# The next batch's Mamba preparation moved from the FFN to the end of attention, 16 scan halves in the FFN, and the squares summed by VectorE

## The reference, cut to what matters

```python
# x (4, 512, 512), ctx (4, 512, 256); every norm is a layernorm without weights
attn = softmax(q k^T / sqrt(32)) v @ Wo   # 16 heads, mixed with a "splat" term from distances to 8 points per head
x1 = layernorm(x + attn)
# cross part, a Mamba scan over the context; 512 channels, 16 states
u = silu(causal_conv4(in_proj @ ctx) + conv_b)
dt_lo, Bm, Cm = split(x_proj @ u)         # 16 + 16 + 16 rows
delta = softplus(dt_proj @ dt_lo + dt_bias)
for n in range(16):                       # per channel, a scan over 512 steps
    state_n[t] = exp(delta[t] * A_n) * state_n[t-1] + delta[t] * u[t] * Bm[n, t]
    y += state_n * Cm[n]
x2 = layernorm(x1 + (y + D * u) * silu(x1))
h = silu(x2 @ Wg) * (x2 @ Wu)             # 2048 wide, ternary weights
out = layernorm(x2 + rms_norm(h) @ Wp)
```

## Time and profile before

| | us |
|---|---|
| median of three runs (lowest, highest) | 1603.4 (1598.43, 1607.87) |
| the profiled execution | 1601.84 |
| its span, first to last instruction | 1599.4 |
| mean granted clock of TensorE | 0.845 of full |

### The profile page before, as it was taken

The page is one execution under the profiler, slowest core; times in us unless marked ns, Lnnn a source line. Parts: engine busy times, 40 slices in busy tenths (PEclk is TensorE's granted clock), DMA queues, the critical chain, the costliest instruction groups (busy, mean ns, idle before and its releaser), DMA issues.

```text
span 1599.4 us, 14040 instructions
## 1 busy us (share of the span) xinstructions
PE 1217.3 (76%) x4602; PEld 571.0 (36%) x4602; DVE 1214.2 (76%) x1425; ACT 744.9 (47%) x1102; POOL 256.7 (16%) x299
## 2 busy tenths in 40 slices
PE   5664747779599857789689858788889856776895
PEld 4332212223345413333445423233445422222453
DVE  5868978789829895789739885889649886889423
ACT  6674424434457533444467423444376424443231
POOL 1000222001112231001112231011112221001111
PEclk8766976779799988789899977889799978788798
DMA  6843893556249795456259793455249693555253
GB/s 195 277 156 105 185 225 88 119 127 136 72 120 213 172 216 143 93 118 133 79 126 214 165 224 115 104 125 134 66 124 230 155 212 103 114 121 114 66 140 90
DMA packets 116759, 228.54 MB, mean 143 GB/s; under 512 B 14560, under 2 KB 25312, under 8 KB 116688
## 3 DMA queue, kind: packets, MB, share of 16 engines
q1 hardware_dynamic: 89248, 144.95, 31.6%
q0 software_dynamic: 26496, 81.80, 26.9%
q10 hardware_dynamic: 944, 0.92, 0.2%
HBM read 116.08 MB, written 29.62 MB: 91 GB/s over the span
## 4 chain that ended last, share of the span: by engine, by line
DVE 32%; PE 27%; DMA 17%; issue 8%; ACT 4%; SPq 2%; POOL 1%; DVEq 0%; ACTq 0%; POOLq 0%
DVE ST L854 10%; PE ps L1432 8%; DMA qk_parts<-PT 5%; DVE ST L846 5%; PE ps L1402 5%; PE ps L1240 4%; DVE MX L910 4%; DMA RD<-PT 4%; DMA RD<-QAK 3%; PE ps L1257 3%; DVE ST L857 3%; DVE BST L890 2%; DMA KS<-qk_parts 2%; DMA YA<-ST 2%; SPq L349 2%
## 5 line engine op out<-in xcount | busy, mean ns | idle before, releaser
L854 DVE TENSOR_TENSOR_SCAN ST<-dA,ST 128x1024 f32<-128x1024 f32 x128 | 316.5, 2473 | 14.9 <-ACT dA L556 11.5
L1240 PE MATMUL ps<-KS,QS 96*128 96x512 f32 x256 | 139.7, 629 | 150.2 <-DVE MX L910 78.3
L910 DVE TENSOR_REDUCE MX<-ps 128x1 f32<-128x512 f32 x256 | 165.0, 685 | 110.6 <-PE ps L1240 110.5
L1432 PE MATMUL ps<-V,GU 128*128 128x512 f16 x1024 | 241.3, 391 | 6.4 <-DVE V L1031 5.6
L457 POOL DMA_DIRECT2D YA<-ST x128 | 112.3, 877 | 790.1 <-DVE ST L857 765.0
L556 ACT ACTIVATE dA<-DL,Aneg 128x511 f32<-128x511 f32 x256 | 168.8, 713 | 97.0 <-DVE ST L854 96.7
L687 ACT ACTIVATE PT<-ps 128x1024 f32<-128x1024 f32 x128 | 125.2, 1019 | 124.2 <-PE ps L1346 123.5
L846 DVE TENSOR_TENSOR ST<-DU,BC 128x1024 f32<-128x1024 f32 x128 | 155.8, 1217 | 13.4 <-DMA BC<-bc_rows 8.0
L857 DVE TENSOR_TENSOR ST<-ST,BC 128x1024 f32<-128x1024 f32 x128 | 159.4, 1245 | 4.4
L1402 PE MATMUL ps<-WP,QS 128*128 128x512 f32 x512 | 144.7, 426 | 14.7 <-DVE QS L1045 13.0
L1240 PEld LDWEIGHTS ps<-KS,QS 96*128 96x128 f32 x256 | 61.3, 256 | 251.1 <-DVE MX L910 136.3
(11 more groups left out here) (224 smaller groups left out, 1623.1 us busy)
## 6 DMA issues: line engine op xcount, KB each, us to landing
YA<-ST POOLq DMA_DIRECT2D x128, 512.0 KB, 7.5
BC<-bc_rows SPq DMA_DIRECT2D x64, 512.0 KB, 5.9
qk_parts<-PT SPq DMA_DIRECT2D x64, 256.0 KB, 6.6
GU<-gu_tiles SPq DMA_DIRECT2D x64, 256.0 KB, 3.4
WP<-proj_tiles SPq DMA_DIRECT2D x64, 256.0 KB, 2.8
QS<-qk_parts SPq DMA_DIRECT2D x48, 256.0 KB, 5.4
KS<-qk_parts SPq DMA_DIRECT2D x48, 256.0 KB, 6.0
RD<-PT POOLq DMA_DIRECT2D x28, 256.0 KB, 5.1
```

Source lines behind the costliest of these rows:

```text
L854: nc.vector.tensor_tensor_scan(flat, dA[:, a, :, :].rearrange("p e s -> p (e s)"), flat, 0.0, ALU.mult, ALU.add).then_inc(s_scan, 1)
L910: nc.vector.tensor_reduce(MX[:, j % 2, qt, h:h + 1], ps[:, n % 2, :], AX_X, ALU.max).then_inc(s_mx, 1)
L1240: mm(ps[:, n % 2, :], QS[i][0:3 * D, h, qt * P:(qt + 1) * P], KS[i][0:3 * D, h, :], start=True, stop=True).then_inc(s_xs, 1)
L1432: last = mm(ps[:, f % F_RING, :], GU[:, t % GU_RING, k, m * P:(m + 1) * P], XHL[:, z, k, :], start=(k == 0 and z == 0), stop=(k == KT - 1 ...
```

## The change

- HALVES_EARLY is 16: tiles 1 to 16 of an FFN carry a half of the next batch each. In the attention of batches 1 to 3 remain 16: seven at places 4, 5, 6, 7, 8, 10 and 12, then 2, 3, 3, 1 in the head groups and none behind. Batch 0 keeps its 32.
- The preparation's first part moves to head group 3 of the attention before: context transposes at kt = 0, input projections at kt = 1 and 2, three `conv` at kt = 3 and one behind normalise(3). Its banks are 2 and 3, so the scores of this group have one pair of banks, 4 and 5, and each pair of heads waits for the exponentials of the pair before. The last batch keeps two pairs.
- The second part stands between attention and FFN: Silu, x and dt projections (four banks), Abs and relu, softplus, with its end on VectorE just ahead of tile 0. Only the skip term stays in the FFN, in tiles 0 and 1.
- U and XP of batches 1 to 3 lie in W, in place of Wk and Wq, CT in QAK[1:3]. Wq and Wk are loaded again in every FFN, in eight DMAs of 256 KB in tiles 5 to 12 on SP; the q and k projections wait for them. The store of B and C and the first load of them move from tile 4 to tile 0 on SP, ahead of x.
- Squares: tile 0's by GpSimd into RD; those of tiles 1 to 15 stay ScalarE's, and VectorE adds each to RD, right behind the low part. The accumulating DMAs are gone, and one column product for each row block ends the sum.

```diff
-HALVES_EARLY = 9
+HALVES_EARLY = 16
...
+POOL_SQUARES = 1
...
+        def U(bb):
+
+            return PT[:, 0, :, :] if bb == 0 else W[:, 1, :, :]
+
+        def XP(bb):
+            return PT[:, 1, :, :] if bb == 0 else W[:, 0, :, :]
+
+        def CT(bb):
+            return QAK[:, 3:5, :] if bb == 0 else QAK[:, 1:3, :]
+
+        def ctx_bank(bb, k):
+            return ps[:, (6 if bb == 0 else 2) + k, :]
+
+        def in_bank(bb, e):
+            return ps[:, (6 if bb == 0 else 2) + e % 2, :]
+
+        def xd_bank(bb):
+            return ps[:, 6 if bb == 0 else 4, :]
+
         def dt_bank(bb, e):
-
-            return ps[:, 6 + e % 2 if type(bb) is int and bb == 0 else F_RING, :]
-
-        def ctx_bank(bb, k):
-            return ps[:, (6 if type(bb) is int and bb == 0 else 4) + k, :]
-
-        def xd_bank(bb):
-            return ps[:, 6 if type(bb) is int and bb == 0 else F_RING, :]
-
-        def in_bank(bb, e):
-            return ps[:, 6 + e % 2 if type(bb) is int and bb == 0 else 4 + (2 + e) % 4, :]
+            return ps[:, 6 + e % 2 if bb == 0 else (5, 6, 7, 4)[e], :]
+
+        def score_bank(b, j, h):
+
+            return 4 + h % 2 if j == NG - 1 and b + 1 < B else 2 + h
...
-        PROJ_PLACES = (*range(4, 13), 14)
+        PROJ_PLACES = (4, 5, 6, 7, 8, 10, 12)
...
-            upto = [len(rest) * share // 14 for share in (0, 3, 6, 9, 12, 14)]
+            upto = [len(rest) * share // 14 for share in (0, 3, 6, 9, 12, 14)] if first else (0, 2, 5, 8, 9, 9)
...
+            def reload_weights(bb, i):
+                m, k = divmod(i, KT)
+                if m == 0:
+                    sp.wait_ge(s_cv, 3 * KT * (bb + 1))
+                else:
+                    sp.wait_ge(s_du, bb + 1)
+                    sp.wait_ge(s_ya, KT * (bb + 1))
+                    sp.wait_ge(s_xd, bb + 1)
+                sp.dma_start(W[:, m, k, :], (Wq, Wk)[m][k * P:(k + 1) * P, :]).then_inc(s_W, 16)
...
                     if not last:
                         if t == 0:
-                            load_x(b + 1)
-                        if t == 4:
                             store_bc(b + 1)
                             load_bc(b + 1, 0)
+                            load_x(b + 1)
                         load_next_bc(b + 1, tile_halves(t))
+                        if 5 <= t < 5 + 2 * KT:
+                            reload_weights(b + 1, t - 5)
...
-                    if 0 < t < NT - 1:
-                        pool.wait_ge(s_sq, NT * b + t + 1)
-                        since(pool, s_acc, sums_landed(b, t - 1))
-                        nc.gpsimd.dma_start(RD[:, :], squares(t), accum_op=ALU.add).then_inc(s_acc, 16)
+                    if t < POOL_SQUARES:
+                        pool.wait_ge(s_h, NT * b + t + 1)
+                        if t > 0:
+                            pool.wait_ge(s_acc, NT * b + t)
+                        dst = RD[:, :] if t == 0 else SQ[0]
+                        nc.gpsimd.tensor_tensor(dst, HT[:, t % 2, :], HT[:, t % 2, :], ALU.mult).then_inc(s_sq, 1)
+                        pool.wait_ge(s_sq, POOL_SQUARES * b + t + 1)
+                        if t == 0:
+                            pool.sem_inc(s_acc, 1)
+                        else:
+                            nc.gpsimd.tensor_tensor(RD[:, :], RD[:, :], SQ[0], ALU.add).then_inc(s_acc, 1)
...
+                        if j == NG - 1 and not last:
+                            if kt == 0:
+                                prep_context(b + 1)
+                            if kt in (1, 2):
+                                prep_in(b + 1, 2 * kt - 2)
+                                prep_in(b + 1, 2 * kt - 1)
...
-                    prep_context(b + 1)
+                    for e in range(KT):
+                        prep_u(b + 1, e)
                 for i, r in enumerate(ROWS1):
                     act.wait_ge(s_lnx, 3 * KT * b + i + 1)
                     nc.scalar.activation(V[:, r, :], X1[:, r, :], ACT.Silu).then_inc(s_z, 1)
+                    if i == 1 and not last:
+                        prep_xd(b + 1)
                 if not last:
                     for e in range(KT):
-                        prep_in(b + 1, e)
+                        prep_abs(b + 1, e)
+                    load_exp_ln()
+                    softplus_exp(b + 1)
+                    softplus_ln(b + 1)
...
                 def square(t):
-                    if t > 2:
-                        act.wait_ge(s_acc, sums_landed(b, t - 2))
-                    nc.scalar.square(squares(t), HT[:, t % 2, :]).then_inc(s_sq, 1)
+                    if t >= POOL_SQUARES:
+                        act.wait_ge(s_acc, NT * b + max(t - 1, POOL_SQUARES))
+                        nc.scalar.square(SQ[t % 2], HT[:, t % 2, :]).then_inc(s_sqa, 1)
...
-                        if t == 0:
-                            prep_u(b + 1, 0)
-                            prep_u(b + 1, 1)
-                        if t in (1, 2):
-                            prep_u(b + 1, t + 1)
-                        if t == 3:
-                            prep_xd(b + 1)
-                        if t in (3, 4):
-                            prep_skip(b + 1, 2 * (t - 3))
-                            prep_skip(b + 1, 2 * (t - 3) + 1)
-                        if t in (4, 5):
-                            prep_abs(b + 1, 2 * (t - 4))
-                            prep_abs(b + 1, 2 * (t - 4) + 1)
-                        if t == 5:
-                            softplus_exp(b + 1)
-                        if t == 6:
-                            softplus_ln(b + 1)
+                        if t in (0, 1):
+                            prep_skip(b + 1, 2 * t)
+                            prep_skip(b + 1, 2 * t + 1)
...
+                                if not last:
+                                    for e in range(KT - 1):
+                                        conv(b + 1, e)
...
                 add_splat(b, 3)
+                if not last:
+                    conv(b + 1, KT - 1)
...
+                if not last:
+                    for e in range(KT):
+                        relu_dt(b + 1, e)
...
-                    conv(b + 1, 0)
-                    conv(b + 1, 1)
+                    softplus_end(b + 1)
...
+                    if t >= POOL_SQUARES:
+                        dve.wait_ge(s_sqa, (NT - POOL_SQUARES) * b + t - POOL_SQUARES + 1)
+                        dve.wait_ge(s_acc, NT * b + t)
+                        nc.vector.tensor_tensor(RD[:, :], RD[:, :], SQ[t % 2], ALU.add).then_inc(s_acc, 1)
...
+                    if r == 2 * KT and b > 0:
+                        pe.wait_ge(s_W, 64 + 16 * 2 * KT * b)
...
-                                pe.wait_ge(s_exp, 2 * KT * NG * b + s - 1)
+                                one_pair = j == NG - 1 and not last_batch
+                                pe.wait_ge(s_exp, 2 * KT * NG * b + (s if one_pair else s - 1))
...
+                            if not last_batch:
+                                prep_context(b + 1)
...
+                        if j == NG - 1 and kt in (1, 2) and not last_batch:
+                            prep_in(b + 1, 2 * kt - 2)
+                            prep_in(b + 1, 2 * kt - 1)
...
+                    prep_xd(b + 1)
                     for e in range(KT):
-                        prep_in(b + 1, e)
+                        prep_dt(b + 1, e)
...
-                        pe.wait_ge(s_xp, 2 * KT * (b + 2))
+                        pe.wait_ge(s_abs, KT * (b + 2))
+                        pe.wait_ge(s_rel, KT * (b + 2))
...
+                pe.wait_ge(s_acc, NT * (b + 1))
                 for r in range(KT):
-                    mm(ps[:, 3, r:r + 1], RD[:, r * P:(r + 1) * P], ones[:, 0:1], start=True, stop=False)
-                    last = mm(ps[:, 3, r:r + 1], squares(NT - 1)[:, r * P:(r + 1) * P], ones[:, 0:1], start=False, stop=True)
+                    last = mm(ps[:, 3, r:r + 1], RD[:, r * P:(r + 1) * P], ones[:, 0:1], start=True, stop=True)
                 last.then_inc(s_rms, 1)
```

More of the change, by code:

```diff
@@ L272, in decoder_layer @@
         GU_USES = NT // 2
-        def squares(t):
-            return RD[:, :] if t == 0 else SQ[t % 2]
-        def sums_landed(b, t):
-            return 16 * (NT - 2) * b + 16 * t
         def gu_loaded(b, t):
@@ L562, in prep_context @@
                     act.wait_ge(s_ct, KC * bb + k + 1)
-                    nc.scalar.copy(CT[:, k, :], ctx_bank(bb, k)).then_inc(s_ctc, 1)
+                    nc.scalar.copy(CT(bb)[:, k, :], ctx_bank(bb, k)).then_inc(s_ctc, 1)
             def prep_in(bb, e):
@@ L568, in prep_in @@
                 bank = in_bank(bb, e)
-                nc.scalar.copy(XP[:, e, :], bank).then_inc(s_xp, 1)
-                nc.scalar.activation(U[:, e, :], bank, ACT.Identity, bias=chan[:, 0, e:e + 1],
+                nc.scalar.copy(XP(bb)[:, e, :], bank).then_inc(s_xp, 1)
+                nc.scalar.activation(U(bb)[:, e, :], bank, ACT.Identity, bias=chan[:, 0, e:e + 1],
```

(26 more changed lines are left out.)

40 lines of the change are left out of this document (8 added, 32 removed).

## The result

| | before | after |
|---|---|---|
| median, us | 1600.91 | 1581.94 |
| lowest to highest | 1595.47 to 1607.87 | 1579.22 to 1584.74 |
| span of the profiled execution | 1599.4 | 1580.8 |
| mean granted clock | 0.845 | 0.848 |

The ratio of the times is 0.9892, with a 95% interval of 0.9861 to 0.9924: faster by 1.1%, which is small but clear of the noise. Run once more beside other kernels, it was 0.9901 (0.9873 to 0.9929). The forecast was 1584 us, 19 less than before; the spans differ by 18.6.

The account below looks back on a forecast made before the run. VectorE and TensorE were both busy 76% of the span, so no engine's total decides and each stage was read. Terms -39 + 38 + 6 - 13 - 11 = -19 gave 1584 us against the median 1603.4, range 1560 to 1610.

Parts of the forecast that it names:

- Projections: Projections of batches 1 to 3: three halves fewer give back 13 us a batch, -39 us (-54 to -18).
- End of attention: End of attention, batches 0 to 2: moved preparation and one pair of score banks cost +38 us (+18 to +58).
- the stepping through kt: Head group 3's scores at 0, 4.9, 15.2 and 24.7 us, values done at 30.7, 12 us later than before.
- The clock term: Output products at the end of attention: TensorE idles 4.5 us just before them, its clock falls, adding 2 us.
- theory 1: The forecast's side in the experiments; for one pair of score banks alone, 0 to 3 us a batch.
- Between attention and FFN: Batches 0 to 2: x and dt projections replace input projections and wait for copies and relu, +6 us (0 to +18).
- FFN of batches 0 to 2: Tiles with a half at 6.40 us, a shorter end of the sum, new queue entries covered: -13 us (-20 to +3).
- Last batch: Last batch: no preparation, fewer halves in and behind group 3, FFN additions cost nothing: -11 us (-18 to -4).
- Rival A: Projections: DMA round trips alone bound them, so the gain there is 6 us a batch; 1605 us, chance 0.16.
- B: Head group 3, batches 0 to 2: single pair of score banks delays values, TensorE loses its clock; 1636 us, chance 0.08.
- C: The end of attention is free and the projections give everything: -47 us, 1556 us, chance 0.12.
- D: Whole kernel: VectorE's total decides, 60 additions at 0.60 us cost +36 us; 1639 us, chance 0.02.

Follow-up runs that it names:

- the seven-places run: The kernel before, with seven halves at the projections of batches 1 to 3 and the other three behind normalise(3): 1594.64 us, ratio 0.9980.
- the two runs on the additions: The kernel before with VectorE adding the squares, nothing moved: 1609.32 us, ratio 1.0071; the change without VectorE's additions to RD: 1563.28 us, ratio 0.9794.

## Why the prediction was right, point by point

The forecast of 1584 us stands 2 above the measured median, and the sum of -19 agrees with the spans' 18.6. The mechanism held in its main terms: halves came out dear at the projections, the moved preparation dear at the end of attention, and the additions cost only where VectorE sets the pace. The terms didn't come out as well as their sum:

1. *Projections*, forecast -39, measured -47.7 (-16.2, -12.7, -18.8). The mechanism was right, and the seven-places run shows it by itself. The term was too small: I took 13 a batch out of 6 to 18, where it was 16 on average.
2. *End of attention*, forecast +38, measured +42.0 (20.3, 10.9, 10.8 against 17.5, 10.3, 10.3). Counted from group 3's first scores in batch 1, the stepping through kt gave normalise(3) at 37.6 us, and it came at 38.6; the last addition at 49.3 to 51.3, and it came at 52.1. In batch 0 the last addition came at 65.5 (63 forecast), in the last batch at 31.8 (31). The clock term was right in kind: 3.6 us of idling, then output products 1.7 us longer, and the granted clock in the window 762 to 772 is 0.83. What the forecast weighed badly is the part of the single pair: the run on it alone costs 14 us over three batches in that stage where theory 1 had 0 to 9.
3. *Between attention and FFN*, forecast +6, measured +10.2. By batch: 3.1, 4.2 and 2.9 against 1.3, 2.4 and 2.4. The step that failed in batch 0 is that the projections are under the halves. The x projections are, but the dt projections wait for the copy XD, which stands on ScalarE behind two Silus, and these behind VectorE's late additions:

```profile
424.21 7.19 PE L1247 MATMUL ps<-XD,dtT 16*128 16x512 f32 x8 [9.39 <-ACT XD L601]
```

TensorE had idled for 9.4 us, its granted clock from 424.2 to 431.4 was 0.50, and the eight products took 7.2 us (4.25 in batch 1); VectorE's relu steps waited 1.5 us for them. The first addition of y came 9.9 us after the last addition to x in batches 0 and 1, 6.9 before: +2.9 in both. Batch 1's other 1.2 us lie at the FFN's start, where the first HT came 6.3 us after the first gate product instead of 5.1; the granted clock there was 0.59 from 795 to 801, and 0.70 from 778 to 784 before.
4. *FFN of batches 0 to 2*, forecast -13, measured -8.6. The pace of 6.40 was exact. Tile 1 was the miss: 7.9 us, because ScalarE's skip terms, a table load and dA stand ahead of its fp32r copy, a queue that the forecast priced at nothing (the skip terms moved to tile 0 give back 1.2 of the 1.5 us); and batch 2 started from 95.0 instead of 96.6. The end of the rms sum gave 1.3 a batch (1 taken).
5. *Last batch*, forecast -11, measured -10.0, with the additions free as said.

The terms miss by -8.7, +4.0, +4.2, +4.4 and +1.0, 5 in sum; -4.5 us outside the five terms (setup, groups 0 to 2, the last layernorm and stores) make up for it. So the total is nearer than the terms deserve, and that part is luck.

Rival A was wrong for three halves and partly right beyond them. B was right about a cost and wrong about the clock collapsing: from 720.5 to 753, batch 1's scores and values, the granted clock was 0.95. C didn't come. D is refuted by the two runs on the additions, and with it, for this kernel, any pricing of an edit by an engine's total. The Trainium skill's "Perfetto Trace Analysis", section "Identifying the Most-Contended Engine", would optimise VectorE first, and here VectorE went from 76% to 79% busy while the time fell; its next section, "Optimization Strategy", has the most-contended engine change over time in some kernels, and that is what this kernel bears out. The same skill's page "VectorE: DVE Perf Modes", section "The DRAIN you can't avoid", has the next operation wait for the pipe to empty, but lets one that isn't held start earlier. The second is what the trace shows: the addition lasts 0.69 us and the next start is 0.60 after its own, so 0.60 is the price of an addition.

## What to carry to other kernels

A filler job has a price at each place, not one price. Here a scan half, 4.7 us of VectorE's work where GpSimd doesn't stretch its scan, cost 5.3 us at the projections (47.7 / 9) and 2.6 once fewer were left there; 5.0 behind normalise(3), where nothing hides it (15.0 / 3); 1.2 in the FFN, where TensorE had set the pace ((94.5 - 85.8) / 7); and 0.5 to 1.0 in VectorE's waits of group 3 (16.6 us of waits in batch 1), hardly more than the 1.6 us by which the unchanged batch 0 moved, but 3.0 in the last batch, where those waits are only 5.5 us for two halves of 4.7. Before moving setup work to "free" a stage, price the move alone (here some 1.5% lost), and then count what the room lets in. When an engine's additions replace a DMA chain, ask what else those DMAs would have met: the accumulations kept pace in the old kernel, and in the new one they cost some 19 us (ratio 1.0018 against 0.9892 and 0.9901).
